# Filler products on TensorE, hoisted tile offsets and moved preparation in the last expert stage of a fused token, attention, expert and recurrent kernel

## What is computed

```python
h = h + _L0_ffn_ref(_layernorm(h, axis=-1), ...)      # 16 experts
h = h + _L1_attn_ref(_layernorm(h, axis=-1), ...)     # two recurrent layers, 126 steps
h = h + _L1_ffn_ref(_layernorm(h, axis=-1), ...)      # below, 8 experts

def _L1_ffn_ref(x, W1, b1, W2, b2, Wg, bg):
    xf = x.reshape(Bs * Ns, Ds)
    logits = xf @ Wg + bg
    idx = jnp.argmax(logits, axis=-1)
    out = jnp.zeros_like(xf)
    for e in range(num_experts):
        h = jax.nn.relu(xf @ W1[e] + b1[e])
        y = h @ W2[e] + b2[e]
        out = jnp.where((idx == e)[:, None], y, out)
    return out.reshape(Bs, Ns, Ds)
```

## Time and profile before

| | us |
|---|---|
| median of 3 runs | 1029.43 |
| lowest and highest | 1028.53, 1030.56 |
| the profiled execution | 1026.01 |
| its span | 1024.2 |
| mean granted TensorE clock in it | 0.897 of full speed |

### The profile page before, as it was taken

One profiled execution on the slowest core, in us unless ns is written; L12 is line 12 of the kernel. 1 busy time (PEld: TensorE's weight loads), 2 busy tenths in 40 slices (PEclk: granted clock), 3 DMA queues, 4 the chain that ended last, 5 costly groups with the idle time before them and its releaser, 6 DMA issues.

```text
span 1024.2 us, 44515 instructions
## 1 busy us (share of the span) xinstructions
PE 850.1 (83%) x17176; PEld 683.1 (67%) x17176; DVE 755.6 (74%) x3034; ACT 520.8 (51%) x1600; POOL 363.4 (35%) x564
## 2 busy tenths in 40 slices
PE   3567777637899999957899999999999999987195
PEld 1246553524566666634799999999999999955063
DVE  4448996697767767667788888888888888866044
ACT  0445776505666666634355555555555555543083
POOL 0315664486677777720111111111111111101553
PEclk9767999558999999986899999999999999995577
DMA  7700004121122332235200000000000000000313
GB/s 242 280 28 2 0 1 159 62 67 38 46 75 77 91 89 76 51 98 174 66 2 0 0 0 0 0 0 0 0 0 0 0 0 0 0 2 4 83 55 108
DMA packets 30137, 50.64 MB, mean 49 GB/s; under 512 B 7969, under 2 KB 19161, under 8 KB 30074
## 3 DMA queue, kind: packets, MB, share of 16 engines
q1 hardware_dynamic: 23578, 36.95, 11.1%
q0 software_dynamic: 6496, 12.84, 4.7%
HBM read 38.40 MB, written 11.38 MB: 49 GB/s over the span
## 4 chain that ended last, share of the span: by engine, by line
PE 44%; DVE 3%; POOL 2%; issue 2%; DMA 1%; ACT 1%; DVEq 0%; SPq 0%; POOLq 0%; ACTq 0%
PE quad L1435 20%; PE bank L1435 17%; POOL x_scratch L1711 2%; PE quad L1450 1%; PE bank L1450 1%; PE quad L1784 1%; PE bank L1770 1%; PE quad L1723 1%; PE bank L1754 1%; PE bank L1470 1%; PE quad L1787 0%; DVE post L1586 0%; DMA post<-y_scratch 0%; PE bank L1772 0%; ACT post L1544 0%
## 5 line engine op out<-in xcount | busy, mean ns | idle before, releaser
L1435 PE MATMUL quad<-post,area 128*128 128x32 f16 (+1 forms) x7520 | 238.0, 182 | 5.9 <-DVE post L1631 2.5
L1435 PEld LDWEIGHTS quad<-post,area 128*128 128x128 f16 x7520 | 217.9, 97 | 19.7 <-DVE post L1631 6.8
L1435 PE MATMUL bank<-post,area 128*128 128x32 f16 (+1 forms) x6260 | 193.6, 180 | 4.8 <-DVE post L1631 3.3
L1435 PEld LDWEIGHTS bank<-post,area 128*128 128x128 f16 x6260 | 176.6, 96 | 17.5 <-DVE post L1631 3.8
L1403 POOL COPY post<-post 128x32 f32 (+1 forms) x126 | 28.3, 224 | 343.8 <-DVE post L1631 343.8
L1530 ACT ACTIVATE post<-post 128x96 f32<-128x96 f32 x252 | 71.3, 283 | 137.4 <-DVE post L1586 137.4
L1586 DVE TENSOR_REDUCE post<-bank 128x96 f32<-128x192 f32 x378 | 99.1, 262 | 6.5 <-PE bank L1435 5.2
L1586 DVE TENSOR_REDUCE post<-quad 128x96 f32<-128x192 f32 x378 | 99.4, 263 | 4.7 <-PE quad L1435 4.3
L881 POOL DMA_INDIRECT y_scratch<-area x78 | 76.9, 986 | 42.6 <-DVE area L1268 23.5
L1544 ACT ACTIVATE post<-post 128x32 f32<-128x32 f32 x252 | 57.7, 229 | 64.4 <-DVE post L1600 64.4
L876 POOL DMA_INDIRECT area<-x_scratch,area x78 | 78.2, 1002 | 28.3 <-issue 21.0
(11 more groups left out here) (312 smaller groups left out, 1745.2 us busy)
## 6 DMA issues: line engine op xcount, KB each, us to landing
w0s<-in_w SPq DMA_DIRECT2D x12, 768.0 KB
area<-in_rec SPq DMA_DIRECT2D x7, 640.0 KB
post<-y_scratch SPq DMA_DIRECT2D x8, 504.0 KB
area<-in_w SPq DMA_DIRECT2D x4, 768.0 KB
area<-in_f SPq DMA_DIRECT2D x2, 1024.0 KB, 7.5
area<-in_patches SPq DMA_DIRECT2D x1, 1488.4 KB
x_scratch<-post SPq DMA_DIRECT2D x1, 1472.0 KB, 8.5
area<-in_taps SPq DMA_DIRECT2D x1, 1350.0 KB
```

Source lines behind the costliest of these rows:

```text
L1435: mm = pe.matmul(at[0][:, at[1] + out.start:at[1] + out.stop], rec_w[:, w, s, m * P:(m + 1) * P], operand, start=False, stop=False, skip_g ...
```

## The change

- The four GpSimd operations of `ids()` leave step 5 of the recurrence and stand at the head of `last_pool`, behind a wait for the centred blocks of the last norm. SyncE's two stores of blank rows and marks move with them to the head of `last_sp`.
- The high half of the bias row is made by ScalarE ahead of its last output block of the recurrence. The low half, two memsets and the scaled bias are made by VectorE between the centring and the wait for the deviation.
- ScalarE makes the high half of the first expert's weights ahead of the norm's square root (one of eight, `LOW_FIRST`). VectorE makes seven of the eight low halves ahead of the logits (`LOW_AHEAD`) and one behind the routing, where it was four and four.
- Behind its eighth scatter GpSimd writes `warm` and raises a semaphore. TensorE waits for that and then issues 44 products of the 16-bit identity with itself, 512 columns each, into bank 7 (`keep_clock`), ahead of its other waits. Nothing reads the result.
- TensorE reads the 23 offsets into registers ahead of the tile loop rather than one in each turn.

```diff
-        def norm_act(act, tag, dst, banks, e):
+        def norm_act(act, tag, dst, banks, e, between=lambda: None):
...
                 act.activation(sq[:, j, 0:dst[j].shape[1]], dst[j], ACT.Square).then_inc(sg("squared"), 1)
+            between()
             act.wait_ge(sg("variance"), NORM[tag] + n)
...
                                   ).then_inc(sg("centred"), 1)
+            ahead()
             dve.wait_ge(sg("deviation"), STAGES[tag])
...
-            sp.wait_ge(sg("numbers"), NUMBERS + 2)
-            rows = xs_dram.rearrange("(u p) n -> p u n", p=P)
-            sp.dma_start(rows[:, :, 0:ID], blank.rearrange("p (u n) -> p u n", u=1).broadcast_to([P, PADS, ID])
-                         ).then_inc(sg("xs_clear"), 16)
-            sp.dma_start(rows[:, :, ID:XR].bitcast(I32), pad_ids).then_inc(sg("xs_clear"), 16)
...
             for t in range(2 * BEHIND):
                 both(t, t % 4)
-                if t == 5:
-                    ids()
...
             for j in range(NBLK):
+                if j == NBLK - 1:
+                    act.wait_ge(sg("fg_in"), 48)
+                    act.activation(b2[:, :, 0, :], b2_row, ACT.Copy, scale=HID_SCALE * W_SCALE
+                                   ).then_inc(sg("f_high"), 1)
                 act.wait_ge(sg("fc"), j + 1)
...
         def last_sp(sp):
+            sp.wait_ge(sg("numbers"), NUMBERS + 2)
+            rows = xs_dram.rearrange("(u p) n -> p u n", p=P)
+            sp.dma_start(rows[:, :, 0:ID], blank.rearrange("p (u n) -> p u n", u=1).broadcast_to([P, PADS, ID])
+                         ).then_inc(sg("xs_clear"), 16)
+            sp.dma_start(rows[:, :, ID:XR].bitcast(I32), pad_ids).then_inc(sg("xs_clear"), 16)
...
         def last_pool(pool):
+            pool.wait_ge(sg("centred"), NORM["ln4"] + NBLK)
+            pool.memset(blank, 0.0).then_inc(sg("numbers"), 1)
+            pool.iota(pad_ids, [[P, PADS], [0, XR - ID]], base=TOKENS, channel_multiplier=1
+                      ).then_inc(sg("numbers"), 1)
+            pool.iota(xrow[:, :, ID:XR].bitcast(I32), [[SEQ, TILES], [0, XR - ID]], base=0, channel_multiplier=1
+                      ).then_inc(sg("numbers"), 1)
+            pool.memset(ones, 1.0).then_inc(sg("numbers"), 1)
             pool.wait_ge(sg("xs_clear"), 32)
...
                                         xrow[:, t, :], None).then_inc(sg("x1_out"), 16)
+                if t == TILES // 2 - 1:
+                    pool.memset(warm[:, :], 0.0).then_inc(sg("numbers"), 1)
...
+        KEPT = 44
+
+        def keep_clock(pe, out, n):
+            for _ in range(n):
+                pe.matmul(out[:, 0:4 * P], ident16, ident16.rearrange("p (z n) -> p z n", z=1).broadcast_to([P, 4, P]),
+                          start=True, stop=True, skip_group_check=True)
...
+            pe.wait_ge(sg("numbers"), NUMBERS + 5)
+            keep_clock(pe, bank[7], KEPT)
             pe.wait_ge(sg("route_dve"), AFTER["expert1"])
...
-            at_of = {}
+            at_of = [expert_of(i) for i in range(NT1)]
...
                 if i < NT1:
-                    at_of[i] = expert_of(i)
                     up(i, at_of[i])
...
+        LOW_FIRST, LOW_AHEAD = 1, 7
...
         def last_act(act):
-            norm_act(act, "ln4", xn_blocks, LN4_BANKS, 1)
-            act.wait_ge(sg("f_in"), 32)
-            for e in range(E1):
-                act.activation(fw[:, e * F_ROW:e * F_ROW + F0], f_raw[:, e, :], ACT.Copy, scale=W_SCALE
-                               ).then_inc(sg("f_high"), 1)
...
+            def first_halves():
+                act.wait_ge(sg("f_in"), 32)
+                for e in range(LOW_FIRST):
+                    f_high(act, e)
+
+            norm_act(act, "ln4", xn_blocks, LN4_BANKS, 1, first_halves)
+            for e in range(LOW_FIRST, E1):
+                f_high(act, e)
...
         def last_dve(dve):
-            norm_dve(dve, "ln4", st_blocks, xn_blocks, LN4_BANKS)
+            def first_halves():
+                b2_low(dve)
+                dve.memset(tiles1, 0.0)
+                link(dve, dve.memset(taken1[:, EW1:EW1 + E1], 0.0))
+
+            norm_dve(dve, "ln4", st_blocks, xn_blocks, LN4_BANKS, ahead=first_halves)
...
-            for e in range(E1 // 2):
-                f_low(e)
+            for e in range(LOW_AHEAD):
+                f_low(dve, e)
...
-            for e in range(E1 // 2, E1):
-                f_low(e)
...
+            for e in range(LOW_AHEAD, E1):
+                f_low(dve, e)
```

More of the change, by code:

```diff
@@ L390, in norm_act, with norm_dve @@
                            bias=eps[0:32 * n, e:e + 1]).then_inc(sg("deviation"), 1)
-        def norm_dve(dve, tag, src, dst, banks, between=lambda: None):
+        def norm_dve(dve, tag, src, dst, banks, between=lambda: None, ahead=lambda: None):
             n = len(dst)
@@ L1405, in both @@
                                      ).then_inc(sg("hist"), 1)
-            def ids():
-                pool.memset(blank, 0.0).then_inc(sg("numbers"), 1)
-                pool.iota(pad_ids, [[P, PADS], [0, XR - ID]], base=TOKENS, channel_multiplier=1
-                          ).then_inc(sg("numbers"), 1)
-                pool.iota(xrow[:, :, ID:XR].bitcast(I32), [[SEQ, TILES], [0, XR - ID]], base=0, channel_multiplier=1
-                          ).then_inc(sg("numbers"), 1)
-                pool.memset(ones, 1.0).then_inc(sg("numbers"), 1)
             for t in range(2 * BEHIND):
                 both(t, t % 4)
-                if t == 5:
-                    ids()
             with pool.Fori(2, SEQ // 4) as i:
@@ L1801, in last_pe @@
                 if i < NT1:
-                    at_of[i] = expert_of(i)
                     up(i, at_of[i])
                 if i >= DOWN_LAG1:
-                    down(i - DOWN_LAG1, at_of.pop(i - DOWN_LAG1))
+                    down(i - DOWN_LAG1, at_of[i - DOWN_LAG1])
             for t in range(TILES):
@@ L1814, in last_pe, with f_high, f_low, b2_low @@
                     mm.then_inc(sg("out_ps"), 1)
-        def last_act(act):
-            norm_act(act, "ln4", xn_blocks, LN4_BANKS, 1)
-            act.wait_ge(sg("f_in"), 32)
-            for e in range(E1):
-                act.activation(fw[:, e * F_ROW:e * F_ROW + F0], f_raw[:, e, :], ACT.Copy, scale=W_SCALE
-                               ).then_inc(sg("f_high"), 1)
-            act.wait_ge(sg("fg_in"), 48)
-            act.activation(b2[:, :, 0, :], b2_row, ACT.Copy, scale=HID_SCALE * W_SCALE).then_inc(sg("f_high"), 1)
+        LOW_FIRST, LOW_AHEAD = 1, 7
+        def f_high(act, e):
+            act.activation(fw[:, e * F_ROW:e * F_ROW + F0], f_raw[:, e, :], ACT.Copy, scale=W_SCALE
+                           ).then_inc(sg("f_high"), 1)
+        def f_low(dve, e):
+            dve.wait_ge(sg("f_high"), e + 2)
+            high = fw[:, e * F_ROW:e * F_ROW + F0]
+            dve.scalar_tensor_tensor(out=fw[:, e * F_ROW + F0:(e + 1) * F_ROW], in0=f_raw[:, e, :], scalar=W_SCALE,
+                                     in1=high, op0=ALU.mult, op1=ALU.subtract).then_inc(sg("f_low"), 1)
+        def b2_low(dve):
+            dve.wait_ge(sg("f_high"), 1)
+            dve.scalar_tensor_tensor(out=b2[:, :, 1, :], in0=b2_row, scalar=HID_SCALE * W_SCALE, in1=b2[:, :, 0, :],
+                                     op0=ALU.mult, op1=ALU.subtract).then_inc(sg("f_low"), 1)
+            dve.tensor_scalar(f_bias, cols[:, FB1:FB1 + E1 * C1], HID_SCALE, None, ALU.mult).then_inc(sg("f_bias"), 1)
+        def last_act(act):
+            def first_halves():
[5 more added lines that the diff above has]
+                f_high(act, e)
             act.activation(warm[:, :], warm[:, :], ACT.Relu)
@@ L1876, in rows_low @@
                                          op0=ALU.mult, op1=ALU.subtract).then_inc(sg("x16_low"), 1)
-            def f_low(e):
-                dve.wait_ge(sg("f_high"), e + 1)
-                high = fw[:, e * F_ROW:e * F_ROW + F0]
-                dve.scalar_tensor_tensor(out=fw[:, e * F_ROW + F0:(e + 1) * F_ROW], in0=f_raw[:, e, :], scalar=W_SCALE,
-                                         in1=high, op0=ALU.mult, op1=ALU.subtract).then_inc(sg("f_low"), 1)
-            dve.memset(tiles1, 0.0)
-            link(dve, dve.memset(taken1[:, EW1:EW1 + E1], 0.0))
-            dve.tensor_scalar(f_bias, cols[:, FB1:FB1 + E1 * C1], HID_SCALE, None, ALU.mult).then_inc(sg("f_bias"), 1)
-            for e in range(E1 // 2):
-                f_low(e)
+            for e in range(LOW_AHEAD):
+                f_low(dve, e)
             taken_tiles = taken1[:, 0:EW1].rearrange("p (t e) -> p t e", t=TILES)
```

3 lines of the change are left out of this document (removed).

## The result

| | before | after |
|---|---|---|
| median, us | 1028.98 (4 runs, 1028.14 to 1030.56) | 1019.61 (4 runs, 1017.54 to 1020.15) |
| the profiled execution, us | 1026.01 | 1019.26 |
| its span, us | 1024.2 | 1017.4 |
| granted TensorE clock | 0.897 | 0.904 |

The ratio is 0.9899, 95% interval 0.988 to 0.9917: 9.4 us less. Against the 1029.43 of the prediction that is 1019.0, where 1022.7 was forecast and the range ended at 1019.2. The direction was right and the gain was two fifths larger than forecast, 9.4 to 6.7 us. That is 0.2 us outside the range, less than the interval of the ratio, which on the same base runs from 1017.1 to 1020.9.

A forecast was written before the change was run, and what follows sets the result against it. Bounds: TensorE's serial recurrence, then sixteen GpSimd scatters, the load and 23 tiles. 3.56 + 1.55 + 1.1 + 0.5 = 6.7 us off 1029.43 gave 1022.7 us; 8-in-10 range 1019.2 to 1026.5.

The forecast's parts named there:

- The stop in the recurrence: TensorE's 2.39 us wait on "issue", read as instructions queued behind the store; moving the store takes back 3.56 us.
- Rival 2: The recurrence's stop stays, belonging to the loop entry, or recurs in the norm: 3.56 us missing, 1026.3 us; chance 0.18.
- The move itself: Store and GpSimd operations at about 923: store lands by 935, before its first reader; risk to norm and logit products priced 0.
- The weight halves: Moved halves fit VectorE's and ScalarE's waits at no cost; scatter 2 shortens by about 1.75 us, scatter chain net 1.55.
- the memset: GpSimd's extra memset between two scatters, on the chain: a cost of 0.20 us, from 0.1 to 0.5.
- The offsets: Tile loop without offset loads: 0.08 us less per tile, step 1.62 to 1.54, 14 tiles, 1.1 us (0 to 3.5).
- Rival 4: The 23 offsets don't stay in registers: the 1.1 us is missing, 1023.8 us; shares the forecast's chance of 0.42.
- The reads ahead: The 23 loads ahead of the tile loop cost 1.8 us on TensorE's sequencer, beside the fillers or the load's wait.
- rival 3: Fillers outlast the wait at the tile loop's head; tile 0 is 5.6 to 9.3 us later, 1029 to 1032; chance 0.10.
- the signs that I had named for being wrong: Tile 0 later than the load's landing, the recurrence's stop staying, or a tile step near 1.3 us.
- The fillers and the clock: Ahead of tile 0: clock rises 4.5 us into the fillers, likely falls again around the first tiles; worth 0.5 us.
- Rival 1: The clock holds through the first tiles: it gives 1.7 us in place of 0.5, so 1021.5 us; chance 0.22.

The follow-up runs named there:

- group B: The measurements, on chips numbered 1 and 4, in which the kernel before takes 1072 to 1076 us.
- group A: The measurements, on chips numbered 8, 9 and 1, in which the kernel before takes 1027 to 1029 us.
- the run that held the clock: The changed kernel with the offset reads ahead of the fillers and 52 fillers for 44: 1017.63 us, ratio 0.9891 to the kernel before.
- the halved reads: The changed kernel with offsets of tiles 0 to 10 read ahead, 11 to 22 each in its turn: 1069.75 us, ratio 0.9933, in group B.

## Why the prediction was wrong

**The stop in the recurrence: right.** 3.44 us of the 3.56 came back, and moving the store alone does it. The packets of instructions bear out the reading that they queued behind the store. Rival 2 is out. By the Trainium skill ("Runtime: NRT & Kernel Launch", section "Instruction fetch mechanics") a taken branch can force a fetch; the traces show the loop's entry at nothing in most kernels with the store gone, and at 0.4 to 0.9 us in three of them (the first seven copies take 20.27 to 20.79 us there, 19.9 in the others), not at 2.39. The chance of 0.18 that I left it was fair for what the trace before held, as it could not separate the two.

**The move itself: right.** The two stores are issued at 924.69 and 925.10, nothing waits for them, and TensorE's norm and logit products show no stop on "issue". Two of the four GpSimd operations take 0.36 and 0.35 us and not 0.20, which costs nothing there.

**The weight halves: right, with less cover than I counted.** They went at nothing, but only just:

```profile
931.74 4.29 DVE L1838 SCALAR_TENSOR_TENSOR post<-area,post 128x512 f16<-128x512 f32 x7
936.31 0.29 DVE L1920 TENSOR_TENSOR area<-quad,post 126x128 f32<-126x128 f32 x1 [0.28 <-PE quad L1735]
```

0.28 us of the wait for the logits are left, where 0.8 to 1.1 were counted, as the logits came sooner than before. An eighth low half would have been on the path. On the chain of scatters they gave 1.77 us rather than 1.55: the excess went as forecast, and the memset was priced at 0.20 and costs 0. The Trainium skill ("GPSIMD Engine Reference", section "1. Specifications") says that GpSimd contends with VectorE instructions that have two inputs in SBUF; the low halves are such, and this case agrees, with scatter 2 at 2.82 or 2.83 us beside four of them and 1.02 where the only one ends 0.16 us after the scatter begins.

**The offsets: the step that failed.** The price of a read was wrong: 0.08 us where it is 0.36. I compared two short gaps on TensorE's products, 0.37 and 0.23 us, and took what was left after one product for the read, with 0.25 us as the upper bound. One gap shows the sequencer's time only in part, since the products behind it come late as well. A tile of the kernel before:

```profile
996.70 0.29 PE L1754 MATMUL bank<-const,post 128*128 128x128 f16 x2
997.01 0.23 PE L1770 MATMUL bank<-area,post 128*128 128x128 f16 x1
...
997.13 0.23 PE L1772 MATMUL bank<-area,post 128*128 128x128 f16 x1
997.26 0.23 PE L1770 MATMUL bank<-area,post 128*128 128x128 f16 x1
...
997.52 0.23 PE L1772 MATMUL bank<-area,post 128*128 128x128 f16 x1
```

From the transposes to the first up product it is 0.31 us here and 0.12 in after. From the first of the six up products to the last it is 0.51 here and 0.29 in after, evenly spaced. The sequencer's own rows give the price directly, and the trace before had them: a read takes 0.30 us, the instruction behind it starts 0.06 later, and the reads of the kernel before are 1.58 to 1.80 us apart behind 988. At this point the sequencer has nothing stored up, so all of a read counts: 1.62 − 0.36 = 1.26 us, which is the step after. Below that nothing goes, since the sequencer's other work for a tile, ScalarE and GpSimd all take 1.24 to 1.26. The quick tiles, 1.09 us at 976, are no sign that TensorE could go faster; its sequencer takes 1.26 for that turn too, and the products come from what it had stored up. 14 tiles at 0.36 us are 5.0 us; the whole chain gave 6.1 to 6.9. Rival 4 is out, since the row after counts 23 reads, all ahead of the loop. The Trainium skill (the same page and section as above) gives about 200 ns for a register load, in a passage on the register traffic that the runtime adds. The traces have 0.30 for the load and 0.36 for what it takes of the stream, and the measurement decides; by the page's figure my estimate was 2.8 us, nearer than the 1.1 of the sum but short of the 5.0.

**The reads ahead: the same price, once more.** I put 23 × 0.08 = 1.8 us of them beside the fillers, at no cost. That they would run there was right: they begin at 962.0, 3.8 us ahead of the last filler's end, when the sequencer has handed on the fillers that stand before them. At 0.08 us they would have been done by 963.8. At 0.37 they take 8.5 us and end at 970.5, which is 3.2 us after tile 0 could have started. That is rival 3's mechanism with another length: tile 0 came late, though by the reads and not by the fillers, and the gain in the loop outweighed it. Two of the signs that I had named for being wrong came true, tile 0 behind the landing of the load and a tile step near 1.3 us, and both go back to this price. With the right one, the order of two blocks in TensorE's stream would have stood out as the thing to ask about.

**The fillers and the clock: right.** The rise came at 958.5, 4.6 us into them, and it fell again before tile 0. In the other runs looked at it came 3.1 to 4.7 us into them. The windows of after:

```profile
957.00:958.00 1.00, 1.00 (x4) 0.30 (x2) 0.00 (x0) 0.00 (x0) 0.69 (x2) 0.50 0.06 15
958.00:959.00 1.00, 1.00 (x5) 0.43 (x4) 0.00 (x0) 0.00 (x0) 0.80 (x1) 0.77 0.23 69
...
968.00:969.00 1.00, 0.00 (x0) 0.00 (x0) 0.00 (x0) 0.00 (x0) 0.00 (x0) 0.85 1.10 318
...
975.00:976.00 1.00, 1.00 (x12) 0.61 (x11) 0.83 (x2) 0.97 (x5) 0.00 (x0) 0.74 0.00 0
```

The first three tiles ran at the low level and the clock was back by 976. 0.5 us were forecast, 0.7 are there, and even those are not the fillers' for certain: without them the kernel is the same within what can be measured, and its clock rose 5.7 us behind the start of tile 0, where after has 5.0. So the number came out near by luck as much as by reason. Rival 1 did not come about, and the run that held the clock puts it at 0.5 to 1.0 us, where I had 1.2: a loop that the sequencer, ScalarE and GpSimd hold makes little use of the faster clock.

**Not in the sum: 1.8 us ahead of the first scatter.** The clock fell during the norm in both kernels, 10.6 us behind the last history copy before and 13.8 after, so more of the norm's and logits' products ran at the high level. Over the 18 traces the stretch took 26.1 to 28.1 us with no pattern by edit, but with one by the clock: where it fell after 10.6 us and stayed low the stretch took 28.0 to 28.1 us, where it fell after 13.2 to 13.9 us 26.1 to 26.8. The kernel before with the store at step 60 has 26.1 and none of the moved preparation. It is a matter of when the clock falls, and I would not count it for the change.

**The balance.** 3.5 + 1.8 + 6.9 + 0.7 − 3.2 = 9.7 us, with the recurrence's rest and the norm (0.6 + 1.8) left out as unexplained, against 9.4 measured by the medians. One wrong price entered twice, with opposite signs: the reads in the loop were worth 5.0 to 5.8 us more than the forecast had, and the same reads ahead of the loop cost 3.2 us that it had at nothing. That the forecast came within 0.2 us of its range is owed to this. In group B the kernel gains 3 to 4 us; the sum without the loop is 2.8, which fits a loop that gives nothing there. One sum of the prediction is off besides: the far end of rival 3 adds up to 1033 us and not 1032, and nothing hangs on it.

The better order is in the runs: the reads ahead of the fillers. In group B that is 5.4 us less in one comparison (intervals apart) and 1.95 in the other (not apart). In group A its ratio of 0.9896 can't be told from the 0.9899 of the changed kernel.

## What to carry to other kernels

Look for the sequencer's own rows before pricing what it does: here a register load took 0.30 us and 0.36 of the stream, and no gap between two products showed that. Where the sequencer has nothing stored up, that whole time comes off the step when the load leaves the loop, down to what the next engine needs. When such loads are moved ahead of a loop, they are a block in a stream like any other, 8.5 us for 23 of them; put them in front of what waits, not behind it. A large store may delay an engine that doesn't touch its data: a stop on "issue" while the DMA queues are full is worth a run with the store moved by some steps.

## What the hardware showed beyond what was expected

- The store at step 5 stops TensorE for 2.39 us and costs 3.5; the same store at step 60 costs nothing. Packets of instructions pass at step 5, 2 us late, and none pass at step 60.
- A register load on TensorE takes 0.30 us, and 23 of them follow each other every 0.37 us. TensorE's sequencer gets ahead of its products: the first load behind the fillers began while 3.8 us of them were still to run.
- A memset of 128x1 between two indirect DMAs is free: the gap of 0.30 us holds it.
- Indirect DMAs follow each other at 0.96 + 0.30 = 1.26 us on GpSimd, which bounds a loop with one per tile.
- The same program takes 4 to 5% longer in some measurements than in others. The difference is not spread evenly: 38 to 45 us lie in the first expert stage and 7 to 8 in the last loop of the changed kernel, in which every third tile comes 1.2 us late, while the recurrence behind its fifth step took 397.9 to 399.1 us on either. Taking the reads out of the loop gave 6.1 to 6.9 us in the one group and, as far as the medians and the halved reads tell, nothing in the other.
